# Reordering the first three tiles of a four-layer kernel on all queues

## What is computed

```python
x = x + L0_ffn(L0_cond(x, cond_128, ...), base_W, gate_W, lora_A, lora_B)   # conv 9 taps; base + 28 LoRA experts, top 2
x = x + L1_ffn(L1_cond(x, cond_128, ...), w, b)                              # mixed 32x32 weights; fake-quantised linear
x = x + L2_ffn(L2_cond(x, cond_128, ...), W_gate, W_up, W_down)
x = x + L3_ffn(L3_cond(x, cond_128, ...), gate_w, gate_b, w1, b1, w2, b2)

# L0_ffn
base = xf @ base_W.T; logits = xf @ gate_W.T
top_vals, top_idx = top_k(logits, 2); top_probs = softmax(top_vals)
h = einsum("nd,erd->ner", xf, lora_A) * (gate_full * 2.0)[:, :, None]
out = base + einsum("ner,eor->no", h, lora_B)

# L1..L3 cond: a small MLP of cond_128 gives softmax scores, which mix 8 weight sets
att = softmax(gelu(gelu(e @ W0 + b0) @ W1 + b1) @ W2 + b2)
out = einsum("boi,bih->boh", einsum("bk,koi->boi", att, weight), x) + (att @ bias_k)[:, :, None]

# L1_ffn: both operands rounded to integers of 8 bits with a scale per row
scale = max(max_abs / 127, 1e-8); q = clip(round(v / scale), -128, 127) * scale
```

## Time and profile before

| | us |
|---|---|
| median of 3 runs | 745.34 (744.99 to 745.41) |
| the profiled execution | 744.57 |
| its span in the profile | 742.8 |
| TensorE busy in the span | 730.5 (98%) |
| VectorE busy | 461.3 (62%) |
| GpSimd busy | 343.6 (46%) |
| ScalarE busy | 300.2 (40%) |

### The profile page before, as it was taken

How to read it: one execution, slowest core, us unless ns; L and a number is a source line. 1 busy time by engine, 2 the same in 40 slices (tenths; PEclk the granted TensorE clock), 3 DMA queues, 4 the chain that set the end, 5 groups by cost and what they waited for, 6 DMA issues and landing times.

```text
span 742.8 us, 11107 instructions
## 1 busy us (share of the span) xinstructions
PE 730.5 (98%) x3595; PEld 593.1 (80%) x3595; DVE 461.3 (62%) x1060; ACT 300.2 (40%) x577; POOL 343.6 (46%) x382
## 2 busy tenths in 40 slices
PE   8899999999999999999999999999999999999997
PEld 5687777877788888888888888877788887888886
DVE  4976667678622345763477345886688887755533
ACT  5644445444432333254334334232555334534321
POOL 3556677676425522121221015867655645464540
PEclk9999999999999999999999999999999999999999
DMA  8666447544051022110220102513513211221200
...
DMA packets 44775, 68.91 MB, mean 93 GB/s; under 512 B 21248, under 2 KB 21600, under 8 KB 44464
## 3 DMA queue, kind: packets, MB, share of 16 engines
...
q10 hardware_dynamic: 752, 0.74, 0.3%
...
## 4 chain that ended last, share of the span: by engine, by line
PE 82%; POOL 7%; DVE 4%; issue 3%; DMA 3%; ACT 1%; SPq 0%; POOLq 0%; DVEq 0%; ACTq 0%
PE bank L2224 21%; PE bank L2207 13%; PE bank L2175 12%; PE bank L2080 10%; PE bank L1865 8%; PE bank L1796 4%; PE bank L1901 3%; POOL wur L692 2%; PE bank L2186 2%; PE bank L1935 2%; DMA tap<-in_x_taps_dram 1%; POOL wgr L690 1%; PE bank L1913 1%; PE bank L2100 1%; PE bank L2037 1%
## 5 line engine op out<-in xcount | busy, mean ns | idle before, releaser
L1648 DVE TENSOR_TENSOR sil<-bank,sil 128x512 f32<-128x512 f32 x56 | 38.6, 689 | 96.5 <-PE bank L2224 96.5
L2224 PE MATMUL bank<-th,wgr 128*128 128x512 f32 x224 | 88.2, 394 | 1.0 <-DVE tl L1436 1.0
L2224 PE MATMUL bank<-th,wur 128*128 128x512 f32 x224 | 87.6, 391 | 0.0
L2080 PE MATMUL bank<-wda,hh 128*128 128x512 f32 x224 | 87.5, 391 | 0.0
L2224 PE MATMUL bank<-tl,wgr 128*128 128x512 f32 x224 | 87.3, 390 | 0.0
L2224 PE MATMUL bank<-tl,wur 128*128 128x512 f32 x224 | 87.2, 389 | 0.0
L2080 PE MATMUL bank<-wda,hl 128*128 128x512 f32 x224 | 87.2, 389 | 0.0
L2175 PE MATMUL bank<-wda,xch 128*128 (+1 forms) x272 | 84.6, 392 | 0.0
L1103 ACT ACTIVATE hh<-sil 128x512 fp32r<-128x512 f32 x56 | 35.4, 632 | 113.0 <-DVE sil L1648 113.0
L1095 ACT ACTIVATE sil<-bank 128x512 f32<-128x512 f32 x56 | 33.4, 597 | 96.6 <-PE bank L2224 96.5
L1650 DVE TENSOR_TENSOR hl<-sil,hh 128x512 fp32r<-128x512 f32 x56 | 46.8, 835 | 39.1 <-ACT hh L1103 39.1
...
## 6 DMA issues: line engine op xcount, KB each, us to landing
...
xres<-xd SPq DMA_DIRECT2D x4, 1024.0 KB, 5.5
xd<-xres SPq DMA_DIRECT2D x4, 1024.0 KB, 5.3
tsd<-tf SPq DMA_DIRECT2D x4, 1024.0 KB, 4.3
...
```

The source lines that it names most:

```text
L1648: v.tensor_tensor(hf[:, m % 2], p_pre[(2 * m + 1) % 3][:], sil[:, m % 2], ALU.mult).then_inc(s_hf, 1)
L2080: last = mm(p_acc[j][:], h[:, m % HSLOTS, j * P:(j + 1) * P], wda[:, m * D:(m + 1) * D], start=(m == 0 and n == 0), stop=(m == MT - 1 and ...
L2224: last = mm(p_pre[(2 * m + b) % 3][:], w[:, (m * KT + kt) * P:(m * KT + kt + 1) * P], x[:, kt], start=(kt == 0 and n == 0), stop=(kt == KT ...
```

## The change

All edits are in the first three tiles, save for the order of matmuls within `conv` and `lora`, which holds for all 16. Nothing is computed that wasn't before, and nothing is left out; 9 of the 25 filler matmuls go (14, 4, 4, 3 become 12, 2, 2, none).

- SP's loads: `ga_raw` goes to second place; the four MLP loads come from ScalarE's queue to the place behind it, and the three of `d_cond` go to ScalarE's queue; tap tile 1 goes ahead of `w0_raw`, the first mix block behind it, tap tile 2 and `xin` of tile 0 ahead of the wait for that block.
- TensorE: `conv` is ordered by parts (three shifts of high by high, three of high by low, three of low by high) and waits for each operand where it is first used; the bias matmul (`side_scale`) runs inside conv(0). router(0) goes ahead of scores. `mixing_weights` and `mixed(0)` go into step 1, `mixed(1)` behind base(1), `mixed(2)` behind hidden(1), `mix1(0)` and `weights_t` into step 2 behind router(2). `scales_t` writes bank 4 instead of bank 6. `lora` is ordered by parts as well.
- ScalarE: `w0_hi(0)` goes ahead of `hid2`; an `Exp` of one column is run early, behind `w0_hi(1)`; the list for tiles 0 and 1 is in a new order; it makes the four copies into `wq` in step 2.
- VectorE: gating(0) goes ahead of the softmax, which is split by `w0_lo`; `softmax_two` and both `mix_rows` go behind `t0_lo(1)`; `weight_scales` goes between gating(1) and gated(1); the copies into `wq` and `weight_integers` are gone.
- GpSimd: the first mix block behind `w0h`; `x1_lo(0)` ahead of the four multiplies; `weight_integers` in four pieces among tile 0's and tile 1's work.

```diff
         d_agg, d_tab, d_b1b = (sem(f"d_{n}") for n in "agg tab b1b".split())
-        s_swt, s_swb = sem("s_swt"), sem("s_swb")
+        s_swt, s_swb, s_mixh = sem("s_swt"), sem("s_swb"), sem("s_mixh")
...
             load_tap(0)
-            sp.dma_start(condt[:], cond_t).then_inc(d_cond, 16)
-            sp.dma_start(cw4[:], cw_t).then_inc(d_cond, 16)
-            sp.dma_start(fs4[:], fside).then_inc(d_cond, 16)
             sp.dma_start(ga_raw[:], l0_ga).then_inc(d_ga, 16)
+            sp.dma_start(mw01[:], mlp_w01).then_inc(d_mlp, 16)
+            sp.dma_start(mw2[:], mlp_w2).then_inc(d_mlp, 16)
+            sp.dma_start(mb01[:], mlp_b01).then_inc(d_mlp, 16)
+            sp.dma_start(mb2[:], mlp_b2.partition_broadcast(BATCH)).then_inc(d_mlp, 16)
+            load_tap(1)
+            sp.dma_start(w0_raw[:], l0_w).then_inc(d_w0, 16)
             sp.dma_start(mixr[:, 0], mix_w[:, 0]).then_inc(d_mix, 16)
-            sp.dma_start(w0_raw[:], l0_w).then_inc(d_w0, 16)
-            load_tap(1)
             sp.dma_start(lb_raw[:], l0_lb).then_inc(d_lb, 16)
+            load_tap(2)
             load_xin(0)
+            sp.wait_ge(d_mix, 16)
+            sp.dma_start(mixr[:, 1:], mix_w[:, 1:]).then_inc(d_mix, 16)
...
             sp.dma_start(b1b[:], l1_b.partition_broadcast(P)).then_inc(d_b1b, 16)
-            load_tap(2)
-            sp.wait_ge(d_mix, 16)
-            sp.dma_start(mixr[:, 1:], mix_w[:, 1:]).then_inc(d_mix, 16)
...
             rounded(gah[:], ga_raw[:], s_gas)
-            pool.wait_ge(d_mix, 16)
-            rounded(mixh[:, 0], mixr[:, 0], s_mix)
...
             rounded(w0h[:, 3], w0_raw[:, 3], s_w0p)
-            pool.wait_ge(s_mix, 2)
+            pool.wait_ge(d_mix, 16)
+            rounded(mixh[:, 0], mixr[:, 0], s_mixh)
...
             pool.wait_ge(d_mix, 32)
-            rounded(mixh[:, 1:], mixr[:, 1:], s_mix)
+            rounded(mixh[:, 1:], mixr[:, 1:], s_mixh)
             tap_lo(2)
+            x1_lo(0)
...
                 nc.gpsimd.tensor_scalar(w1_raw[:, k], w1_raw[:, k], wsc[:, 2, k:k + 1], MAGIC, ALU.mult, ALU.add).then_inc(s_wqf, 1)
-            x1_lo(0)
+            tap_lo(3)
+            def weight_integers(k):
+                pool.wait_ge(s_wqf, k + 1)
+                nc.gpsimd.tensor_scalar(wq_rows[:, k], w1_raw[:, k], MAGIC, QMAX, ALU.subtract, ALU.min).then_inc(s_wqr, 1)
+            weight_integers(0)
+            weight_integers(1)
             diag_tile(0)
+            weight_integers(2)
             diag_lo(0)
-            tap_lo(3)
+            weight_integers(3)
...
             act.dma_start(conv_raw[:], conv_w).then_inc(d_conv, 16)
-            act.dma_start(mw01[:], mlp_w01).then_inc(d_mlp, 16)
-            act.dma_start(mw2[:], mlp_w2).then_inc(d_mlp, 16)
-            act.dma_start(mb01[:], mlp_b01).then_inc(d_mlp, 16)
-            act.dma_start(mb2[:], mlp_b2.partition_broadcast(BATCH)).then_inc(d_mlp, 16)
+            act.dma_start(condt[:], cond_t).then_inc(d_cond, 16)
+            act.dma_start(cw4[:], cw_t).then_inc(d_cond, 16)
+            act.dma_start(fs4[:], fside).then_inc(d_cond, 16)
...
                                      bias=mb01[:, l, 0:1]).then_inc(s_g1, 1)
+            def w0_hi(k):
+                nc.scalar.activation(w0h[:, k], w0_raw[:, k], ACT.Copy).then_inc(s_w0s, 1)
             t0_hi(0)
+            tap_hi(1)
+            act.wait_ge(d_w0, 16)
+            w0_hi(0)
...
                                      bias=mb01[:, l, 1:2]).then_inc(s_g1, 1)
-            tap_hi(1)
-            def w0_hi(k):
-                nc.scalar.activation(w0h[:, k], w0_raw[:, k], ACT.Copy).then_inc(s_w0s, 1)
+            w0_hi(1)
+            nc.scalar.activation(rt[:, 192:193], ones[:, 0:1], ACT.Exp)
...
                 diag_hi1(t - 1)
+                if t == 2:
+                    for k in range(KT):
+                        act.wait_ge(s_wqt, k // 2 * 2 + 2)
+                        nc.scalar.activation(wq[:, k], bank[6 - k // 2][:].bitcast(BF16)[:, (k % 2) * D:(k % 2 + 1) * D],
+                                             ACT.Copy).then_inc(s_wqc, 1)
...
                     act.wait_ge(s_swt, 1)
-                    nc.scalar.activation(swb[:], bank[6][:], ACT.Copy).then_inc(s_swb, 1)
+                    nc.scalar.activation(swb[:], bank[4][:], ACT.Copy).then_inc(s_swb, 1)
...
+            gate_exp(0)
...
             nc.scalar.activation(atte[:], att[:], ACT.Exp).then_inc(s_g1, 1)
-            act.wait_ge(d_w0, 16)
-            w0_hi(0)
-            gate_exp(0)
-            w0_hi(1)
+            act.wait_ge(d_lb, 16)
+            nc.scalar.activation(lbh[:], lb_raw[:], ACT.Copy).then_inc(s_lbs, 1)
...
             nc.scalar.activation(identb[:], ident[:], ACT.Copy).then_inc(s_atc, 1)
+            hidden_hi(0)
+            t0_hi(1)
+            tap_hi(2)
...
                                  ACT.Copy).then_inc(s_atc, 1)
-            act.wait_ge(d_lb, 16)
-            nc.scalar.activation(lbh[:], lb_raw[:], ACT.Copy).then_inc(s_lbs, 1)
-            t0_hi(1)
-            hidden_hi(0)
+            x1_hi(0)
+            gate_exp(1)
+            conv_out(2)
             mixed(0)
-            tap_hi(2)
+            tap_hi(3)
             mixed(1)
-            gate_exp(1)
-            x1_hi(0)
-            conv_out(2)
             mixed(2)
-            tap_hi(3)
-            diag_hi1(0)
...
             hidden_hi(1)
+            diag_hi1(0)
...
-                dve.wait_ge(s_mix, done)
+                dve.wait_ge(s_mixh, done)
...
-            mix_rows(slice(0, 1), 1)
             t0_lo(0)
...
                 gating(t, t - 2 if t >= 2 else None)
+                if t == 1:
+                    weight_scales()
                 gated(t)
-                if t == 1:
-                    weight_integers()
...
                     t0_lo(t + 1)
-                if t == 1:
-                    for k in range(KT):
-                        dve.wait_ge(s_wqt, k // 2 * 2 + 2)
-                        v.tensor_copy(wq[:, k], bank[6 - k // 2][:].bitcast(BF16)[:, (k % 2) * D:(k % 2 + 1) * D]).then_inc(s_wqc, 1)
...
-            def weight_integers():
-                for k in range(KT):
-                    dve.wait_ge(s_wqf, k + 1)
-                    v.tensor_scalar(wq_rows[:, k], w1_raw[:, k], MAGIC, QMAX, ALU.subtract, ALU.min).then_inc(s_wqr, 1)
+            w0_lo(0)
+            w0_lo(1)
+            gating(0, None)
+            w0_lo(2)
             softmax_one()
-            softmax_two()
-            gating(0, None)
-            for k in range(KT):
-                w0_lo(k)
+            w0_lo(3)
...
             t0_lo(1)
-            mix_rows(slice(1, COND_LAYERS), 3)
-            weight_scales()
+            softmax_two()
+            mix_rows(slice(0, 1), 1)
+            mix_rows(slice(1, COND_LAYERS), 2)
...
-            def conv(t):
-                pe.wait_ge(s_tapl, t + 1)
+            def conv(t, between=None):
+                pe.wait_ge(s_taph, t + 1)
+                pe.wait_ge(s_cvw, 1)
...
                     pe.wait_ge(s_cvs, t)
-                n = 0
-                for s in range(SHIFTS):
-                    for w, x in parts((cvh[:, s], cvl[:, s]), (taph[:, :, s:s + P], tapl[:, :, s:s + P])):
-                        last = mm(p_cv[:].rearrange("p (b n) -> p b n", b=BPT), w, x, start=(n == 0), stop=(n == 3 * SHIFTS - 1))
-                        n += 1
+                for n, (w, x) in enumerate(((cvh, taph), (cvh, tapl), (cvl, taph))):
+                    if n == 1 and between:
+                        between()
+                    if n == 1:
+                        pe.wait_ge(s_tapl, t + 1)
+                    if n == 2 and t == 0:
+                        pe.wait_ge(s_cvw, 2)
+                    for s in range(SHIFTS):
+                        last = mm(p_cv[:].rearrange("p (b n) -> p b n", b=BPT), w[:, s], x[:, :, s:s + P],
+                                  start=(n == 0 and s == 0), stop=(n == 2 and s == SHIFTS - 1))
...
             pe.wait_ge(s_junk, 1)
-            keep_busy(14)
-            pe.wait_ge(s_cvw, 2)
-            conv(0)
-            pe.wait_ge(d_cond, 48)
-            mm(bank[7][:, 0:BATCH], cw4[:], condt[:], start=True, stop=True).then_inc(s_m1, 1)
+            def side_scale():
+                pe.wait_ge(d_cond, 48)
+                mm(bank[7][:, 0:BATCH], cw4[:], condt[:], start=True, stop=True).then_inc(s_m1, 1)
+            keep_busy(12)
+            conv(0, side_scale)
...
                 mm(bank[5][:, l * BATCH:(l + 1) * BATCH], mw01[:, l, 0], condt[:], start=True, stop=True).then_inc(s_m1, 1)
-            keep_busy(4)
+            keep_busy(2)
...
                 mm(bank[6][:, l * BATCH:(l + 1) * BATCH], mw01[:, l, 1], hid1[:, l], start=True, stop=True).then_inc(s_m1, 1)
-            keep_busy(4)
+            keep_busy(2)
...
-                pe.wait_ge(s_mix, 2 if l == 0 else 4)
+                pe.wait_ge(s_mix, 1 if l == 0 else 2)
...
-                pe.wait_ge(s_htl, t + 1)
-                if t == 0:
```

(43 more changed lines are left out.)

## The result

The kernel after took 749.42 us (median of four executions, 748.86 to 749.91), the kernel before beside it 745.16 (744.45 to 745.41): a ratio of 1.0056, with a 95% interval of 1.0039 to 1.0073. The forecast was 745.4 with a range up to 748.3, so the kernel is slower where no change was expected, and outside the range. The profiled execution took 749.64 with a span of 747.9.

What follows compares the result with a forecast made beforehand. VectorE, up to tile 1's `hm`, was taken to bound the start. Shift of base(2): (33.25 − 33.76) − 1.0 for lora(1) + 1.57 for mix1(0) and weights_t = +0.05; 745.34 + 0.05 = 745.4 us, range 743.4 to 748.3.

Steps and rivals of the forecast that it cites:

- The bound and the prize: In the start VectorE, not TensorE, is tight behind 18.7 us; a new order can win 6 to 7 us, under 1%.
- Parts 1 and 2, loads and tile 0: `w0_raw` lands at 12.9 us; router(0) starts near 12.2, router(1) near 22.4, 3 to 4 us earlier than before.
- Part 3, tile 1's `hm`: VectorE writes tile 1's gated hidden values at 33.25 us, against 33.76 before; bounds 31.0 and 35.1.
- rival A: Less contention: VectorE slips into GpSimd's gaps, `hm` comes at 31.0 to 32.1, time 743.1 to 744.2; chance 0.23.
- Part 4, lora(1): TensorE starts lora(1) at 36.1 us, 2.83 behind tile 1's `hm` instead of 3.83, idling nearly 2 us before it.
- Part 4, GpSimd: GpSimd's queue finishes `diag_lo(0)` at 38.1, the last rounding at 38.8, router(2) ends at 38.9: cover 0.1 to 0.8 us.
- a stall in the pair that just fits: TensorE stalls at mix1(0) and weights_t behind router(2); no chance of its own, within the 0.22 for slower.
- Part 4, "wq copies end 43.2, at nothing": ScalarE's four `wq` copies, 0.55 us each, end near 43.2, wanted at 45.9, so they delay nothing.
- Part 5: Waits inside the matmul groups of conv and lora cost nothing over all 16 tiles; bound 0.3 us.
- Rival B: TensorE falls to half clock after idling ahead of lora(1), costing 2.7 us up to base(2): 748.1; chance 0.11.
- What would show it: Signs: router and `hm` times, base(2) at 43 ± 1; wrong if clock falls before 50 us or TensorE waits between router(2) and base(3).
- The lock of the ports: VectorE and GpSimd share one port pair, locked for a whole instruction; gated(1) beside GpSimd's multiplies therefore kept at 3.04 us.

Runs made afterwards that it cites:

- e3: Kernel after, with the rounding into `wq_rows` back on VectorE behind gated(1) and fillers (5 and 8) in TensorE's two idle stretches: 747.93 us, ratio 1.0022.
- e10: e9 with ScalarE doing `t0_hi(2)` and `hidden_hi(1)` ahead of the copies of mixed(2): 745.48 us, ratio 0.9993.
- e9: Kernel after, with GpSimd's four roundings as multiply by one and add of minus the constant, limit at 127 left out: 747.93 us, ratio 1.0018.
- e1: Kernel after, with only the rounding into `wq_rows` back on VectorE behind gated(1): 747.06 us, ratio 1.0012.
- e2: Kernel after, with only filler matmuls added, 5 ahead of hidden(1) and 8 behind mixed(2): 753.01 us, ratio 1.0085.

## Why the prediction was wrong, point by point

- **The bound and the prize.** Right. VectorE was tight up to tile 1's `hm` (busy 9.53 of 10 us from 20 to 30 in the kernel after), the change brought that `hm` forward by 1.34 us and lora(1) by 2.35, and no version gained more at layer 2 than e3's 0.39.
- **Parts 1 and 2, loads and tile 0.** Right on the whole: `w0h` was begun at 12.71, so `w0_raw` was there a little before the 12.9; `mb2` held nobody; router(0) started at 13.07 (forecast 12.2: TensorE waited 0.97 us for `fs` inside conv(0), a load that the prediction didn't look at), router(1) at 22.54 (22.4).
- **Part 3, tile 1's `hm`.** Written at 32.42, forecast 33.25, inside the bounds, between the forecast and rival A's 31.0 to 32.1. gated(1) took 2.68 us (29.74 to 32.42) with steps of 0.56 to 0.63 beside the multiplies; kept at 3.04. The cast in gating(1), feared at 1.3, ran in 0.17 before `x1_lo(0)`. The wait ahead of hidden(1) was 1.30, not 2.4: `hm` came 0.8 earlier, and TensorE had work 0.4 longer.
- **Part 4, lora(1).** Right: 2.82 us behind `hm`, forecast 2.83, with a wait of 2.0, as forecast, that copies and `t0_hi(2)` cause. e10 showed that this order was a choice worth 1.8 us at lora(1).
- **Part 4, GpSimd: the step that failed.** "Two integer roundings (priced as its multiply, 0.68)", and with it "mix1(0) and weights_t just fit". Each took 1.92, so four end at 42.93 instead of 38.8, and `diag_lo(0)` at 40.92 instead of 38.1. The 0.1 to 0.8 us of cover was gone several times over. Two faults are in that step. Different operations of one shape were given one price, without a bound from above, where the nearest row for one was at hand: GpSimd's subtraction of the same width at 1.29 would have given four roundings 4 × (1.29 − 0.68) = 2.4 us more and a stall of some 1.6. And a thin cover was counted as nothing, while its miss stood in "a stall in the pair that just fits", at a few hundredths of the chance. With e9's price, 0.62, the rest of the step holds: table at 36.3 (forecast 36.5), `bd1l` done at 37.7. Without the step's error the time comes back into the range: 747.93 in e9, 747.06 in e1.
- **The account of base(2).** lora(1) −2.35; owed mix1(0) and weights_t +1.57; half clock in lora(1) and router(2) +1.47; waits of 1.24 and 1.02, +2.26; the remaining +0.54 lies mostly around these waits, which the list counts shorter than the gaps between matmuls are (1.40 and 1.18 beyond the usual step). Sum +3.49. The clock's 1.47 is no loss on top: in e2, without it, the wait for `diag_lo(0)` was 2.75 and mix1(0) started no earlier. Then hidden(2) +0.40, as `x1_bias(0)` and with it tile 2's `hm` were late, and conv's order +0.37: 4.26. Taken one by one from the kernel after, the roundings are worth 2.45 at layer 2 (e9), and roundings and clock together 4.64 (e3): they overlap.
- **Part 4, "wq copies end 43.2, at nothing".** They ended at 48.28, with `x1h` ahead of them waiting for VectorE; the same cause.
- **Part 5.** Wrong in size: conv's order, with its wait, costs 0.03 us a tile, 0.37 over twelve, just above the bound of 0.3. It was argued from one pair of matmuls across a wait in base(0), which has no conv in it.
- **Rival B** was the better rival than its 0.11 said. Its mechanism came in the kernel after itself, at the place named, and its price agrees with what e1 and e3 differ by at base(2) (2.7 forecast, 2.70). That is in part luck: the prediction set the half clock for half of the work without a row that said so, and counted only the 5.35 us of work of the old order. In the profiled execution of the kernel after 1.47 of it is there, hidden behind GpSimd.
- **What would show it.** Both alarms named, the clock below 1.00 before 50 us and a wait between router(2) and base(3), went off.
- **The lock of the ports**, on which Part 3 rested (the Trainium skill, "SBUF — State Buffer", section "SBUF: two separate sides"), is seen again near 505 us, at 1.34 against 0.23 us for one instruction. There e3's chain lost 3.3 us beside GpSimd's work, more than its lead of 0.39 at layer 2. At the start it cost less than was priced: gated(1) took 2.68.
